# One more round of lead for the maxima of an attention kernel, and another order of its heads

## What is computed

```
q = split_heads(x @ w_q); k = split_heads(text @ w_k); v = split_heads(text @ w_v)
out_text = softmax(q k^T / 4) v                 # over 1593 tokens
out_ip   = softmax(q k_ip^T / 4 + mask) v_ip    # over 8 tokens
out = (out_text + out_ip) @ w_out + b_out + x
```

## Time and profile before

| what | value |
|---|---|
| median of 3 runs | 1841.28 us (1838.55 to 1843.44) |
| the profiled execution | 1848.91 us |
| its span, first to last instruction | 1847.0 us |
| PE busy | 1811.4 us, 98% |
| DVE, ACT, POOL busy | 72%, 64%, 21% |
| mean granted clock of the PE | 0.993 |
| chain that ended last | PE 93%, DVE 2%, DMA 2% |

### The profile page before, as it was taken

One profiled execution on the slowest core, in us unless ns is written; L12 is line 12 of the kernel. 1 busy time (PEld: TensorE's weight loads), 2 busy tenths in 40 slices (PEclk: granted clock), 3 DMA queues, 4 the chain that ended last, 5 costly groups with the idle time before them and its releaser, 6 DMA issues.

```text
span 1847.0 us, 41069 instructions
## 1 busy us (share of the span) xinstructions
PE 1811.4 (98%) x16856; PEld 718.8 (39%) x16856; DVE 1332.3 (72%) x1787; ACT 1185.7 (64%) x2340; POOL 382.6 (21%) x508
## 2 busy tenths in 40 slices
PE   8999999999999999999999999999999999999988
PEld 3333333433344343433344333343333433434332
DVE  6777777778767787677876777777777777767871
ACT  1276666666666666666666666666666666666766
POOL 5112222211122121122121221112122122221000
PEclk9999999999999999999999999999999999999989
DMA  7555334363344434355453464435544364343410
GB/s 226 102 92 160 67 77 92 73 164 73 74 106 116 106 71 86 94 139 102 79 99 75 141 103 77 97 69 144 94 77 96 72 155 85 74 95 74 77 30 26
DMA packets 103806, 178.16 MB, mean 96 GB/s; under 512 B 42933, under 2 KB 71270, under 8 KB 103618
## 3 DMA queue, kind: packets, MB, share of 16 engines
q1 hardware_dynamic: 82658, 134.12, 37.3%
q0 software_dynamic: 18944, 40.10, 6.9%
q10 hardware_dynamic: 2016, 1.31, 0.2%
HBM read 117.63 MB, written 48.98 MB: 90 GB/s over the span
## 4 chain that ended last, share of the span: by engine, by line
PE 93%; DMA 2%; DVE 2%; SPq 1%; ACT 1%; issue 1%; POOL 0%; ACTq 0%; DVEq 0%; POOLq 0%
PE pv_bank L800 27%; PE max_bank L727 20%; PE work_bank L582 12%; PE exp_bank L784 12%; PE work_bank L604 11%; PE work_bank L627 3%; PE work_bank L593 2%; PE max_bank L745 2%; PE exp_bank L788 1%; DVE tile_max L1069 1%; DMA o_t<-o_sum 1%; SPq L475 1%; ACT probs L978 1%; PE work_bank L658 1%; PE work_bank L611 1%
## 5 line engine op out<-in xcount | busy, mean ns | idle before, releaser
L978 ACT ACTIVATE probs<-exp_bank 128x512 f32<-128x512 f32 x1908 | 1002.0, 599 | 417.3 <-PE exp_bank L784 410.2
L1069 DVE TENSOR_REDUCE tile_max<-max_bank 128x2 f32<-128x1024 f32 x632 | 773.4, 1224 | 400.5 <-PE max_bank L727 395.5
L727 PE MATMUL max_bank<-k_stack,q_stack 48*128 48x512 f32 x1896 | 567.9, 469 | 7.4 <-DVE tile_max L1069 7.3
L800 PE MATMUL pv_bank<-probs,v_ones 128*17 128x512 f32 x3840 | 518.1, 603 | 0.1
L1071 DVE TENSOR_REDUCE tile_max<-max_bank 128x1 f32<-128x512 f32 x632 | 430.2, 681 | 2.7 <-PE max_bank L727 2.7
L784 PE MATMUL exp_bank<-q_stack,k_stack 50*128 50x512 f32 x1908 | 415.9, 403 | 4.0 <-DMA q_stack<-neg_rows 2.7
L727 PEld LDWEIGHTS max_bank<-k_stack,q_stack 48*128 48x128 f32 x1896 | 234.0, 185 | 409.8 <-issue 269.6
L784 PEld LDWEIGHTS exp_bank<-q_stack,k_stack 50*128 50x128 f32 x1908 | 240.0, 188 | 63.2 <-ACT probs L978 47.2
L582 PE MATMUL work_bank<-ctxt,wk 128*32 128x400 f32 x2528 | 253.5, 506 | 7.6 <-DMA wk<-in_w_k 5.5
L604 PE MATMUL work_bank<-wv,ctxt 128*32 128x320 f32 x3040 | 254.0, 435 | 0.0
L604 PEld LDWEIGHTS work_bank<-wv,ctxt 128*32 128x32 f32 x3040 | 93.8, 109 | 163.1 <-issue 100.3
(11 more groups left out here) (124 smaller groups left out, 832.3 us busy)
## 6 DMA issues: line engine op xcount, KB each, us to landing
k_stack<-scratch_k SPq DMA_DIRECT2D x234, 199.2 KB, 6.9
scratch_k<-k_parts SPq DMA_DIRECT2D x80, 400.0 KB, 4.6
ctxt<-in_ctx_t POOLq DMA_DIRECT2D x28, 800.0 KB, 11.1
q_stack<-scratch_q SPq DMA_DIRECT2D x240, 64.0 KB, 2.3
scratch_q<-q_parts SPq DMA_DIRECT2D x80, 128.0 KB, 5.7
r_wide<-scratch_r POOLq DMA_DIRECT2D x39, 256.0 KB, 5.1
xres<-in_x SPq DMA_DIRECT2D x8, 640.0 KB, 9.0
out<-xres SPq DMA_DIRECT2D x32, 160.0 KB, 1.9
```

The costliest lines, as they stand in the source:

```text
L727: nc.tensor.matmul(round_place(n, r)[:, k, :], exact(q_stack[stack, slot, c, t * 128:(t + 1) * 128]), exact(k_stack[stack, slot, c, chunk ...
L800: last = nc.tensor.matmul(pv_bank[h * 32:h * 32 + VW, :], v_ones[:, v_slot(b, kt), head * VW:(head + 1) * VW], p, start=(kt == 0), stop=(k ...
L978: nc.scalar.activation(dst, exp_place(group_no, at), ACT.Exp, scale=SCALE).then_inc(probs_ready, 1)
L1069: nc.vector.reduce_max(flat[:, at:at + 2], place[:, 0:2, :], AX.X).then_inc(max_taken, 1)
```

## The change

`LEAD` becomes 4, so each visit holds the round after the one it held: visits 0 to 12 hold rounds 4 to 16, visit 13 the rest round, visits 14 to 16 rounds 1 to 3. The prologue takes one round more, in the second half of its last K piece. The order of the heads of the exponent tiles becomes (0, 2, 1, 3), sides 0, 1, 0, 1. Nothing else is changed; NEG stays in visit 14, and the pieces and PV stay where they are.

```diff
-HEADS_IN_TURN = (2, 0, 3, 1)
+HEADS_IN_TURN = (0, 2, 1, 3)
...
-LEAD = 3
+LEAD = 4
...
-PRO_PLAN += [(("NEG", 0), ALL, 0)] + [(("K", 2, c), half, 1 - c * n) for c in range(2) for n, half in enumerate(HALVES)]
+PRO_PLAN += [(("NEG", 0), ALL, 0)] + [(("K", 2, c), half, 1) for c in range(2) for n, half in enumerate(HALVES)]
```

## The result

| | before | changed |
|---|---|---|
| median of 5 runs each | 1842.97 us (1838.55 to 1845.27) | 1872.16 us (1870.84 to 1875.64) |
| the profiled execution, its span | 1848.91, 1847.0 us | 1874.9, 1873.1 us |
| PE, DVE, ACT busy | 1811.4, 1332.3, 1185.7 us | 1831.6, 1331.0, 1188.7 us |
| mean granted clock of the PE | 0.993 | 0.992 |

The ratio is 1.0163, 95% interval 1.0146 to 1.018: slower by 29.2 us, 1.6%, between the medians; the forecast was 28.4.

What follows compares the result with a forecast made beforehand. The PE, busy 98%, was taken as the bound, with DVE pacing visits without a piece. Terms 8.0 + 13.0 + 4.0 + 3.0 + 0.4 = 28.4 us took the median from 1841.3 to 1869.7; 8-in-10 range 1854 to 1897.

Steps and rivals of the forecast that it cites:

- Two halves: Visits 14 and 15: third exponent and third maximum share one array half, one such pair more; +0.22 us in 36 groups, 8.0.
- NEG's copy: Visit 14: without the rest to hide ACT's copy of NEG, the next piece waits; net 0.36 us in 36 groups, 13.0.
- 0.77 + 0.01 + 0.87: Visit 14: the PE reaches the piece 1.65 us after the first exponent matmul, so waits 0.55 for ACT's copy.
- Both visits are PE bound: Visits 14 and 15: the PE sets their pace, so the added same-side pair costs 0.22 us in each of 36 groups.
- No gain faces it: Visits 14 to 16 of the kernel before have no idle PE to win back, so nothing offsets the losses.
- The rest's wait for DVE: The rest in visit 13 starts 2.31 us after visit 12's first exponent matmul in g = 1, 3, 4; +4.0 us overall.
- The maxima of visit 14: They wait 0.2 us for DVE's reductions of the rest behind V or OUT pieces, 15 groups: +3.0 us; K pieces none.
- Ends: Prologue's added round costs 1.9 us, group 38 gives back 1.5, groups 1 and 37 cost 0: +0.4 us.
- B, the clock falls too: Rival, 0.12: idle PE in visits 12 to 14 of g = 1 groups drops the clock; 28 us more, 1898.
- C, faster: Rival, 0.04: DVE releases the rest before the PE arrives, 1.8 not 2.3 us after visit 12's first exponent; 1834.9 us.
- D, the copy is met: Rival, 0.09: visit 14's piece does not wait for NEG's copy; 15.4 us slower instead of 28.4, 1856.7 us.
- No change: Rival, 0.05: waits of the rest's new place equal those of the old, only small parts bite; within 5.5 us.

Runs made afterwards that it cites:

- e5: The changed kernel with the edits of e2, e3 and e4 together: 1841.08 us, 0.9987 of the kernel before.
- e1: The changed kernel with the old order of heads (2, 0, 3, 1), LEAD still 4: 1971.97 us, 1.0705 of the kernel before.
- e3: The changed kernel with the order of heads swapped for the last two key blocks, so visits 14 and 15 use two halves: 1865.41 us.
- e2: The changed kernel with DVE instead of ACT copying the negative rows, ahead of its reductions in visit 14: 1863.41 us.
- e6: The kernel before (LEAD 3), heads (0, 2, 1, 3) for the last key block and the rest's small matmuls' halves in the other order: 1831.04 us.
- e4: The changed kernel with one step of a piece moved from visit 11 to 12 in g = 1, 3 and 4: 1868.4 us.
- e7: e6 with one step of K moved from visit 5 to the empty visit 4 in g = 3 and 4: 1833.19 us.

## Why the prediction was right

**The sum.** 28.4 forecast, 29.2 measured between medians, and the ordinary groups give 27.2 in the profiles where the terms had 28.0. Each kind of group came within 30 ns of its forecast. The interval of the ratio is 27 to 33 us, and the two profiles are 26.0 apart, so agreement to 0.8 us is closer than these runs can tell and partly luck. The lengths of the visits are the better test.

**Two halves (8.0 us) and NEG's copy (13.0 us).** Their sum was right, 0.58 in each group against the 0.57 that e5 takes out of visit 14, and both mechanisms are there: e1 and e3 show the halves, e2 the copy. But they are not two terms to be added. The piece starts when ACT's copy is done, 2.19 after e, whether PV ends at 1.67 (changed kernel) or at 1.45 (e3). So the shared half of visit 14 costs nothing as long as the copy is late, and the copy alone costs the whole 0.56 to 0.58: e2 gives back 0.34, e3 nothing there, e5 0.57. I had measured the copy's wait from a path that held the 0.22 already (the 0.77 in 0.77 + 0.01 + 0.87). That made the sum right; either term by itself, as a price of its own, was not. "Both visits are PE bound" was wrong as it stood: visit 14 is bound by ACT's order, and visit 15 by DVE in g = 0. "No gain faces it" was true of idle PE, but visit 15 of the kernel before held a shared half, and e6 takes 6 us out of it.

**The rest's wait for DVE (4.0 us).** It starts 2.31 after e of visit 12 in g = 1, 3 and 4, to the hundredth as forecast from group 1 of the kernel before. e4 takes the wait away and gets 0.2 per group.

**The maxima of visit 14 (3.0 us).** 0.19 us in group 16, where OUT is the piece, and in all 15 groups with V or OUT: 2.9 us; none in group 18 with K, as forecast. This part was seen in the trace alone, not taken away in a run.

**Ends (0.4 us).** The prologue gave 1.7 of the 1.9. Behind it the clock was at half for 3.4 us from 83 on, which the forecast had not: group 0 took 1.6 more than its kind. Timeline of the PE at the end of the prologue:

```profile
79.74 0.77 PE L727 MATMUL max_bank<-k_stack,q_stack 48*128 48x512 f32 x3
81.59 0.50 PE L727 MATMUL max_bank<-k_stack,q_stack 48*128 48x512 f32 x2 [1.08 <-DVE tile_max L1069]
```

The added round at 79.74, 1.08 us of idle PE, then visit 0. Group 38 gave back 0.6 instead of 1.5, group 1 gave 1.0 where 0 was forecast, and group 37 cost 2.2: a stretch of half clock began there at 1780 and lasted 13.7 us, against 10.2 before. Group 2 was 2.5 us shorter and group 27 1.3, against 0.6 longer for their kind: a stretch of half clock of 6.8 us at the border of groups 1 and 2 was 3.4 after, and one of 3.4 us in group 27 was gone. These differences of the clock are in no term of the forecast; together with group 38 they make up the -2.8 us above.

**The rivals.** B, the clock falls too: the half-clock stretches add up to 31 us in the profiled run, before to 28, and none of the 35 groups from 2 to 36 has one in the changed kernel; the idle 1.3 us of a g = 1 group doesn't bring it about. The rule of the Trainium skill ("TensorE: Matmul & The Clock Gate", "A second HAM failure mode: psum-queue depth-cycling") did not act on these waits: the granted mean went from 0.993 to 0.992. C, faster, fell at its own point, 2.31 and not 1.8. D, the copy is met, fell with the wait of 0.52 in visit 14. No change fell with the interval, and with visits 12 to 14, longer in every kind.

## What to carry to other kernels

Before work is moved out of a full stage, ask what it was hiding there: the rest round in visit 14 covered ACT's three exponentials and the copy behind them, and NEG stayed where the cover had been. A stage with an engine idle is not free for work that must wait for another engine's last result: the visit without PV lies right behind DVE's last round. When two costs end at the same instruction, price the later one, for repairing one may show nothing until the other is repaired.

## What the runs showed of the hardware that was not expected

- Splitting a piece into one more stretch between score matmuls costs about 0.1 us (0.79, 1.48 and 2.15 us for one, two and three steps of K).
- DVE copies the 32 x 128 negative rows in 0.28 us, about as fast as ACT (0.26).
- The stretches of half clock differ from profile to profile: 28 us in the kernel before, 31 in the changed one, 5 and 8 in e6 and e7 (mean clock 0.999 and 0.998). They differ between runs of one kernel as well: in the 17 runs of the kernel before beside e5 to e7 the mean clock went from 0.991 (1849.51 us) to 0.999 (1836.87 us). So one profile of each doesn't show that an edit moved them, and a gain of a few us shouldn't be put down to an edit before the clock is compared.
- Three profiles have a stretch in a middle group, all in visit 2 of g = 2: the kernel before (group 27, from 1285, 3.4 us), e2 and e3 (group 17, from 848 and 847, 6.8 and 3.4 us). In each the PE had stood idle just before, in visit 1, for 1.32, 1.27 and 1.19 us, until ACT had copied a Q piece (the row below is group 27 of the kernel before). This wait is in visit 1 of every g = 2 group from the second batch on, 0.8 to 1.5 us long in the changed kernel and e2, and mostly the clock stays up behind it (e2, group 7: 1.52 us). It was not found out what decides.

```profile
1283.03 0.75 PE L693 MATMUL work_bank<-wout,vip_own 128*32 128x320 f32 x8 [1.32 <-ACT q_full L918]
```
